# Graph attention on one core: sums one quad later and ahead of the expansions, one-hots one step ahead instead of two

## The reference, cut to what matters

```python
def _L1_gnn_ref(h, src, dst, W_qkv, b_qkv, W_out, b_out):      # h 3125 x 256, 50000 edges, sorted by dst, H 8 heads of DH 32
    qkv = (h @ W_qkv + b_qkv).reshape(n, 3, H, DH)
    q, k, v = (qkv[:, 0], qkv[:, 1], qkv[:, 2])
    score = jnp.einsum('ehd,ehd->eh', q[dst], k[src]) * SCALE
    mx = jax.ops.segment_max(score, dst, num_segments=n)
    ex = jnp.exp(score - mx[dst])
    denom = jax.ops.segment_sum(ex, dst, num_segments=n)
    attn = ex / denom[dst]
    msg = attn[:, :, None] * v[src]
    h_new = jax.ops.segment_sum(msg, dst, num_segments=n)
    h_out = jnp.transpose(h_new, (0, 2, 1)).reshape(n, DIM)
    return (h_out + h) @ W_out + b_out
...
x = x + _L0_gnn_ref(_layernorm(x), src, dst, edge_weight, ...)
x = x + _L0_ffn_ref(_layernorm(x)[None], ...)[0]
x = x + _L1_gnn_ref(_layernorm(x), src, dst, ...)
x = x + _L1_ffn_ref(_layernorm(x)[None], ...)[0]
```

## Time and profile before

| | us |
|---|---|
| median of 3 runs | 3851.94 |
| lowest and highest | 3847.45, 3861.17 |
| the profiled execution: its own time | 3869.41 |
| its span in the profile | 3867.0 |
| busy in the span: PE, DVE, POOL, ACT | 2325.9, 1824.8, 1528.6, 831.4 |
| the attention phase, from the first gather to the last addition | 2212 to 3234 |

### The profile page before, as it was taken

The page is one execution under the profiler, slowest core; times in us unless marked ns, Lnnn a source line. Parts: engine busy times, 40 slices in busy tenths (PEclk is TensorE's granted clock), DMA queues, the critical chain, the costliest instruction groups (busy, mean ns, idle before and its releaser), DMA issues. The chain is left out here.

```text
span 3867.0 us, 50211 instructions
## 1 busy us (share of the span) xinstructions
PE 2325.9 (60%) x10567; PEld 1749.9 (45%) x10568; DVE 1824.8 (47%) x4614; ACT 831.4 (22%) x2022; POOL 1528.6 (40%) x1330
## 2 busy tenths in 40 slices
PE   3187877777455310399924746666666765509972
PEld 2165555555234200277712435455445543408960
DVE  5766767575533000100136446566666664424435
ACT  0022222221131000023301133333333331102320
POOL 0078888888501776500020034444444430050022
PEclk7577778787666655699955878888988887559985
DMA  4267777777720201111115334444444441521232
GB/s 189 72 108 128 119 121 121 119 123 117 130 88 10 73 9 53 33 49 49 41 43 162 111 111 128 120 121 123 127 121 129 120 115 38 208 76 59 70 115 66
DMA packets 259048, 378.46 MB, mean 98 GB/s; under 512 B 36563, under 2 KB 196203, under 8 KB 257131
## 3 DMA queue, kind: packets, MB, share of 16 engines
q0 software_dynamic: 110368, 188.67, 24.5%
q1 hardware_dynamic: 134267, 148.92, 12.3%
q10 hardware_dynamic: 14288, 39.59, 2.7%
HBM read 245.59 MB, written 131.47 MB: 98 GB/s over the span
## 5 line engine op out<-in xcount | busy, mean ns | idle before, releaser
L1175 POOL DMA_INDIRECT sum_tab<-Vs,spot x416 | 687.4, 1652 | 170.5 <-issue 105.6
L2202 POOL DMA_INDIRECT KV<-kv_tab,iS x448 | 427.1, 953 | 385.5 <-DVE msg L2302 218.3
L2378 PE MATMUL psO<-msg,hot 128*128 128x264 f32 x896 | 325.8, 526 | 197.7 <-DVE msg L2302 115.1
L1099 PE MATMUL psV<-XN,Bs 128*128 x832 | 332.7, 516 | 182.6 <-issue 176.2
L2378 PEld LDWEIGHTS psO<-msg,hot 128*128 128x128 f32 x896 | 222.9, 261 | 263.9 <-issue 204.9
L1603 PE MATMUL psH<-XNT,W1s 128*128 128x320 f32 x640 | 197.4, 465 | 196.6 <-issue 88.8
L1099 PEld LDWEIGHTS psV<-XN,Bs 128*128 128x128 f32 x832 | 165.9, 240 | 318.5 <-issue 310.9
L1544 POOL DMA_INDIRECT hs<-h_tab,iS x256 | 242.4, 947 | 108.3 <-issue 83.8
L1614 PE MATMUL psY<-W2s,hT 128*128 128x256 f32 x800 | 188.2, 393 | 126.3 <-issue 126.3
L2367 PE MATMUL psQ<-Qs,hotT 128*128 x904 | 229.4, 399 | 39.2 <-ACT hotT L2440 29.1
L2431 ACT ACTIVATE away<-iota_free,dlN 128x128 f32<-128x128 f32 x456 | 145.7, 390 | 492.5 <-issue 264.2
(11 more groups left out here) (526 smaller groups left out, 4389.1 us busy)
## 6 DMA issues: line engine op xcount, KB each, us to landing
kb<-key_rows SPq DMA_DIRECT2D x104, 256.0 KB
sum_tab<-zeros ACTq DMA_DIRECT2D x8, 1664.0 KB, 17.9
parts<-sum_tab SPq DMA_DIRECT2D x20, 640.0 KB
ye_tab<-Ye SPq DMA_DIRECT2D x20, 640.0 KB
Y<-ye_tab SPq DMA_DIRECT2D x20, 640.0 KB
disp_tab<-blank ACTq DMA_DIRECT2D x5, 1792.0 KB
xb<-disp_tab SPq DMA_DIRECT2D x68, 128.0 KB
lowB<-sort_tab SPq DMA_DIRECT2D x27, 320.0 KB
```

The lines of the kernel that those rows point to most:

```text
L1099: ins = nc.tensor.matmul(psV[:, r % 2, x, :], Bs[:, q % 2, 2 * h + x, :], XN[:, bass.ds(t, 1), :].rearrange("p a d -> p (a d)"), start=Tru ...
L1175: pool.indirect_dma_start(out=sum_tabs[k], out_offset=bass.IndirectOffsetOnAxis(ap=spot[:, s, u:u + 1], axis=0), in_=Vs[:, j % VR, :], in_ ...
L2202: pool.indirect_dma_start(out=KV[:, s, u, :], out_offset=None, in_=kv_tab, in_offset=bass.IndirectOffsetOnAxis(ap=iS[:, s, u:u + 1], axis= ...
L2378: ins = nc.tensor.matmul(psO[:, x // 2, 0:AW], hot[:, QU * slot + x, :], msg[:, k % 2, x, :, :].rearrange("p h c -> p (h c)"), start=(x % ...
```

## The change

In words, engine by engine:

- **ScalarE** makes the one-hots of quad k + 1 in step k, not of quad k + 2, and lays those down. The copy of the exponents into `msg` (`sums`) goes to the front of the step, except in step 1, where it stays last behind the exponents. The exponents of step 1 now come behind the laying down of the one-hots.
- **TensorE** transposes the one-hots of quad k + 1, then sums quad k - 6, not k - 5, and then expands. The row ends of step 0 come behind the sums, the turning back of step 1 too, and the columns of step 0 stay last. The tail has a step more.
- **VectorE** takes the maxima ahead of the products in step 1. In every step both additions follow the reduction. Since an addition is that of quad k - 6 as before, it now waits for the sums of its own step, not for those of the step before.
- **POOL** waits, before it issues a quad's gathers, until those of the quad two before have landed.

The diff:

```diff
--- before.py
+++ after.py
@@ -2198,6 +2198,10 @@
                                     k = HP * s + j
                                     if j and not zero(b):
                                         hold(pool, weighed, RING * (b - 1) + k + 1)
+                                    if k >= 2:
+                                        hold(pool, kv_in[k - 2], 16 * QU * (b + 1))
+                                    elif not zero(b):
+                                        hold(pool, kv_in[k - 2 + RING], 16 * QU * b)
                                     for u in range(QU * j, QU * j + QU):
                                         pool.indirect_dma_start(out=KV[:, s, u, :], out_offset=None, in_=kv_tab,
                                                                 in_offset=bass.IndirectOffsetOnAxis(ap=iS[:, s, u:u + 1], axis=0)).then_inc(kv_in[k], 16)
@@ -2309,20 +2313,19 @@
                             summing = began(b, k - LAG - 1)
                             if summing:
                                 t = tiles_of(b, k)
+                            if past and j == 1:
+                                maxima(b, k)
                             if new:
                                 products(b, k)
                             if past and j == 0:
                                 unit_ends(b, k)
-                            if past and j == 1:
-                                maxima(b, k)
-                            if summing:
-                                add(b, k, 0, t[0])
                             if new:
                                 scores(b, k)
+                            if summing:
+                                for x in range(2):
+                                    add(b, k, x, t[x])
                             if past and j == 0:
                                 across(b, k)
-                            if summing:
-                                add(b, k, 1, t[1])
                             if began(b, k - LAG) and (new or k < LAG):
                                 weigh(b, k)
 
@@ -2347,7 +2350,7 @@
                     def _(pe):
                         def turn_hots(b, k):
 
-                            n, at = RING * b + k + 2, (k + 2) % RING * QU
+                            n, at = RING * b + k + 1, (k + 1) % RING * QU
                             hold(pe, hots, n + 1)
                             if later(n, 1):
                                 hold(pe, evac, n)
@@ -2369,13 +2372,13 @@
                             ins.then_inc(expanded, 1)
 
                         def out(b, k):
-                            q, slot = RING * b + k - LAG, (k - LAG) % RING
+                            q, slot = RING * b + k - LAG - 1, (k - LAG - 1) % RING
                             hold(pe, weighed, q + 1)
                             hold(pe, dens, q + 1)
                             for x in range(QU):
                                 if x % 2 == 0 and later(q, 1):
                                     hold(pe, added, 2 * (q - 1) + x // 2 + 1)
-                                ins = nc.tensor.matmul(psO[:, x // 2, 0:AW], hot[:, QU * slot + x, :], msg[:, k % 2, x, :, :].rearrange("p h c -> p (h c)"),
+                                ins = nc.tensor.matmul(psO[:, x // 2, 0:AW], hot[:, QU * slot + x, :], msg[:, (k - 1) % 2, x, :, :].rearrange("p h c -> p (h c)"),
                                                        start=(x % 2 == 0), stop=(x % 2 == 1))
                                 if x % 2:
                                     ins.then_inc(outs, 1)
@@ -2389,42 +2392,41 @@
                                     hold(pe, exd, g - 1)
                                 nc.tensor.transpose(psM[:, 0:P], S[:, o, :, :].rearrange("p i h -> p (i h)"), ident[:, :]).then_inc(rows_s, 1)
                             if new:
-                                expand(b, k)
+                                turn_hots(b, k)
+                            if began(b, k - LAG - 1):
+                                out(b, k)
                             if past and j == 0:
                                 hold(pe, ends, 2 * g)
                                 nc.tensor.matmul(psM[0:1, P:2 * P], F[:, P - 1:P], ident[:, :], start=True, stop=True)
                                 nc.tensor.matmul(psM[0:1, 2 * P:3 * P], R[:, 0:1], ident[:, :], start=True, stop=True).then_inc(rowed, 1)
+                            if past and j == 1:
+                                hold(pe, exps, g)
+                                nc.tensor.matmul(psM[:, 3 * P + 4:3 * P + 4 + H], star[:, 1, :], ident[0:H, 0:H], start=True, stop=False)
+                                nc.tensor.matmul(psM[:, 3 * P + 4:3 * P + 4 + H], star[:, 0, :], diag[:, :], start=False, stop=True)
+                                nc.tensor.transpose(psM[:, P:2 * P], E[:, :], ident[:, :]).then_inc(backs, 1)
                             if new:
-                                turn_hots(b, k)
+                                expand(b, k)
                             if past and j == 0:
                                 hold(pe, carried, 2 * g)
                                 for n in range(2):
                                     ins = nc.tensor.matmul(psM[:, 3 * P + n:3 * P + n + 1], turned[0:1, n, :, :].rearrange("p i h -> p (i h)"), ones[0:1, 0:1],
                                                            start=True, stop=True)
                                 ins.then_inc(cols_s, 1)
-                            if past and j == 1:
-                                hold(pe, exps, g)
-                                nc.tensor.matmul(psM[:, 3 * P + 4:3 * P + 4 + H], star[:, 1, :], ident[0:H, 0:H], start=True, stop=False)
-                                nc.tensor.matmul(psM[:, 3 * P + 4:3 * P + 4 + H], star[:, 0, :], diag[:, :], start=False, stop=True)
-                                nc.tensor.transpose(psM[:, P:2 * P], E[:, :], ident[:, :]).then_inc(backs, 1)
-                            if began(b, k - LAG):
-                                out(b, k)
-                        turn_hots(0, -2)
+                        turn_hots(0, -1)
                         expand(0, -1)
-                        turn_hots(0, -1)
 
                         def body(b):
                             for k in range(RING):
                                 step(b, k)
                         loop(pe, TRIPS, body)
-                        for k in range(LAG):
+                        for k in range(LAG + 1):
                             step(TRIPS, k, False)
 
                     @block.scalar
                     def _(act):
                         def one_hots(b, k):
 
-                            n, at = RING * b + k + 2, (k + 2) % RING * QU
+                            n, at = RING * b + k + 1, (k + 1) % RING * QU
                             if later(n, RING):
                                 hold(act, outs, 2 * (n - RING) + 2)
                             for x in range(QU):
@@ -2433,11 +2435,11 @@
                             a.activation(hot[:, at:at + QU, :], away[:, :, :], ACT.Relu, bias=ones[:, 0:1], scale=-1.0).then_inc(hots, 1)
 
                         def lay_hots(b, k):
-                            n = RING * b + k + 2
+                            n = RING * b + k + 1
                             hold(act, quads, n + 1)
                             if later(n, 2):
                                 hold(act, expanded, n - 1)
-                            a.copy(hotT[:, k % 2, :], psT[:, :]).then_inc(evac, 1)
+                            a.copy(hotT[:, (k + 1) % 2, :], psT[:, :]).then_inc(evac, 1)
 
                         def cut_node(b, k):
 
@@ -2478,21 +2480,22 @@
 
                         def step(b, k, new=True):
                             j, past = k % HP, began(b, k - HP) and (new or k < HP)
+                            summing = began(b, k - LAG)
+                            if summing and j != 1:
+                                sums(b, k)
                             if new:
                                 one_hots(b, k)
                             if past and j == 0:
                                 cut_node(b, k)
-                            if past and j == 1:
-                                exponents(b, k)
                             if new:
                                 lay_hots(b, k)
                             if past and j == 1:
+                                exponents(b, k)
                                 lay_exponents(b, k)
-                            if began(b, k - LAG):
+                            if summing and j == 1:
                                 sums(b, k)
-                        for k in range(-2, 0):
-                            one_hots(0, k)
-                            lay_hots(0, k)
+                        one_hots(0, -1)
+                        lay_hots(0, -1)
 
                         def body(b):
                             for k in range(RING):
```

## The result

| | us |
|---|---|
| before, median of 4 runs (of 3847.45 to 3863.37) | 3856.56 |
| changed, median of 4 runs (of 3765.76 to 3777.95) | 3773.24 |
| ratio, 95% interval | 0.9785 [0.977, 0.980] |
| profiled execution of the changed kernel, span | 3768.0 |

The change is faster by 83 us where 200 were forecast: right in its sign, wrong in its size, and outside the range. Further on this turns out to depend on the chip: on another one the same kernel gains 197 us.

What follows compares the result with a forecast made beforehand. It took a chain of waits, with no engine full, to bound attention. Saving 7.7 us in each of 26 groups gave 200 us, other terms 0: 3652 us from the 3851.9 median, range 3605 to 3740.

Steps and rivals of the forecast that it cites:

- The ring: Attention's per-step wait loop: one-hot slots wait for sums eight quads back; plain steps were to fall from 6.6 to 5.7 us.
- the walk: Step-by-step timing of one changed attention group: closes at 26.2 us, taken as 27.0 against 34.7 before.
- the allowance of 0.8 a group: Added to the walked attention group: 0.4 us for the old groups' mean and 0.4 for unseen issue gaps.
- The clock: TensorE's sums in steps 0 and 1 speed up from 3.6 to 2.0 us, about 3.2 us a group.
- the clock stays low in step 1 or 2: Rival: TensorE's sums stay slow, 1.6 us each; 3735 us with both, 3694 with one; chance 0.22.
- POOL waits for gathers two quads back: POOL's new landing wait in attention finds its count reached: cost 0, bounds -25 to 80 us.
- The code rival: Attention's loop code is fetched again each trip: 13 x 24.9 = 324 us more, 3976 us, slower; chance 0.04.
- for something outside the kernel's own waits, while the gathers flowed: Reading of ScalarE's one 24.87 us stand in the attention phase, used as the price of a code fetch.
- the rival on late gathers: Gathers of step 0's quad come late for attention's products: 3.7 us a group, 96 us, 3748 us; chance 0.06.
- the sum: Whole-kernel total: 200 us saved, other parts at 0, giving 3669 us profiled and 3652 us as median.
- I read the attention phase alone: The prediction's scope: only attention's 1025 us were read, since the change touches nothing else.

Runs made afterwards that it cites:

- e6: The kernel before, with POOL waiting for the gathers of the quad just before at a group's second and third quad and in the first groups; ratio 1.0023, kind B.
- e1: The changed kernel without POOL's landing wait for the gathers two quads back; 3756.72 us, ratio 0.9745 on a chip of kind A.
- e7: e1 gathering 1 KB rows of another table instead of 2 KB rows, so half the bytes; 3291.15 us, ratio 0.9432 on kind B.
- e9: The changed kernel, landing wait kept, gathering 1 KB rows of another table instead of 2 KB rows; 3283.56 us, ratio 0.9414 on kind B.
- e8: The changed kernel, nothing altered, on a chip of kind B; 3288.3 us, ratio 0.9431.
- e3: The kernel before, with POOL waiting for the weighing once per two quads, so eight gathers go back to back; 3951.5 us, ratio 1.0237 on kind A.
- e15: The change with landing waits after every eight gathers in the experts' stage and only ahead of each group's third quad in attention's groups; 3564.64 us, 0.9254, kind A.
- e17: e15's kernel again, on another chip of kind A; 3615.51 us, ratio 0.9319.
- e12: The same kernel as e9, the change with 1 KB rows gathered, on a chip of kind A; 3778.48 us, ratio 0.9791.
- e14: The change, with POOL also waiting for the landing after every four gathers in the first experts' stage; 3595.83 us, ratio 0.9322 on kind A.
- e2: e1 with a pause on POOL after each quad's gathers, a tile fill of 1.37 us that it waits for; 3735.1 us, ratio 0.9677, kind A.
- e18: e1 with two small POOL fills, each waited for, after every four gathers in attention and the experts' stage; 3346.48 us, ratio 0.9583 on kind B.

## Why the prediction was right, and where it was wrong

- *The ring and the walk* were right. On B every step shown is within 0.4 us of the walk, the group is 26.4 (walked 26.2, used 27.0), and the gain is 197 us (200). Even on A steps 1 to 3 of the group shown are as walked. That 197 comes so near to 200 is in part luck: the allowance of 0.8 a group was too large by 0.6, but the old group is shorter on B too (33.9 in e6, 34.7 on A).
- *The clock*: on B the four sums of a quad take 1.95 to 2.02 us in 98 of the 104 steps behind the first exponents. The rival "the clock stays low in step 1 or 2", whose 3735 is nearest to the measured time, happened there in 6 steps, mostly in step 2, at up to 1.4 us each, and not in every group. On A 24 of 104 steps have slow sums, 13 of them step 0. Like the one shown, behind a stall of 4.92 us, 19 of the 24 follow a stall of TensorE of 2.2 us or more: they are mostly an effect of the late completions.
- *POOL waits for gathers two quads back, costed at 0*: near enough. On A some 16 us or nothing (e1), on B nothing that shows (e7 beside e9).
- *The code rival* fell, and so did the reading of the earlier trace rows on which it stood, "for something outside the kernel's own waits, while the gathers flowed". On A the changed kernel has the same stand, and VectorE has one beside it:

```profile
2232.43 0.60 PE L2358 MATMUL psT<-ident,hot 128*128 128x128 f32 x4
2248.03 1.22 DVE L2235 TENSOR_TENSOR KV<-KV,psQ 128x1024 f32<-128x1024 f32 x1 [23.04 <-remote]
2254.96 0.59 ACT L2442 COPY hotT<-psT 128x512 f32<-128x512 f32 x1 [24.79 <-remote]
```

  Both wait for work that TensorE had finished, during the phase's first and longest run of gathers. On B (e8) ScalarE's copy at the same place starts at 1926.70 after a wait of 1.32 us. The code is the same, so it was not a fetch; it was the effect that took the gain, and I had it in a row.
- **The step that failed** is the sentence in the rival on late gathers, "where the trace has gathers back to back without falling behind". It asked only whether gathers land in time (they do) and not what a run of them does to the other engines. A shorter group closes POOL's pauses, 6 long runs become 26, and on A a completion of TensorE is told 2 to 7.5 us late beside them, mostly about 4, with a slow sum in 22 of 26 groups. In the sum, the term is 31.3 - 26.4 = 4.9 us a group, 27 x 4.9 = 132 us, on chips of kind A. It was priced nowhere, neither in the sum nor as a rival. That all of the 4.9 is this effect rests on the comparison of the kinds and on e3; on A itself, the groups of e15 to e17 without a late completion (27.1 to 27.9 on average) point to 3.4 to 4.2 of it.
- *The limit set at the start*, "I read the attention phase alone", hid it. The experts' stage, 53 of 300 us busy beside a stream of gathers and 200 of 200 without, shows it at full size.

The Trainium skill (SBUF — State Buffer, Who interferes with whom) states that "DMA never contends with a compute engine". On B the trace agrees, with TensorE busy 300 of 300 us beside POOL's gathers. On A it does not, with 53 of 300. In attention the transfers' bytes are not the reason (e12); whether it is POOL's issuing or the number of transfers is not shown.

## What to carry to other kernels

Before costing a faster ring, ask which streams become denser when it shortens, and look in every phase of the trace for the place where that density already exists and what stands still beside it. A wait put down to an unknown releaser, while its producer has long ended, is a finding to be explained, not a start-up cost to be set aside; so is one put down to transfers of another phase. Time a version on more than one chip before an experiment's reading is trusted, and time the unaltered change beside each experiment on its chip.

## What was not expected of the hardware

- Chips of one type differ by 10% on one kernel: three took 3855 to 3883 us for the kernel before, three 3485 to 3489. Profiles of the changed kernel (3768 us on A, 3289 on B) show nearly all of the difference beside long runs of POOL's gathers: 299 us arise ahead of attention, with TensorE busy 54 or 56 of 300 us against 300 of 300 in the experts' stage, 23 at the start of attention, and 131 in its groups of 31.2 or 31.3 us against 26.4.
- On the slower kind TensorE's instructions and completions are late while gathers are issued in runs of eight or more (1.5 to 3.6 us between single products, 2 to 7.5 us and mostly about 4 at a completion, 25 us in the longest run), and not in runs of four with a break of 1 us or more (e14 in the experts' stage; in e2 the breaks are 1.6 us or more). What in the chip does this stays open: the traces end at the engines.
- In e2, three of VectorE's copies took 1.35 to 1.63 us beside POOL's fill of 1.37, where the changed kernel's take 0.16 to 0.27. They end together with the fill:

```profile
2648.87 1.63 DVE L2255 COPY low<-Cf 1x8 f32<-1x8 f32 x1
2648.94 1.55 DVE L2257 COPY low<-psM 1x128 f32<-1x128 f32 x1
2649.10 1.37 POOL L2206 MEMSET idle<- 128x1500 f32 x1
2649.14 1.35 DVE L2258 COPY high<-psM 1x128 f32<-1x128 f32 x1
```

  The median over all groups is 1.56 us for the second copy and 1.36 for the third. In e18, whose fills take 0.12 us, the three copies take 0.16 to 0.27 again, so a filler for a pause should be small.
